# x's second chunk issued by ScalarE after its first chunk has landed, in a float32 adapter kernel with LayerNorm

## The reference

```python
h = einsum('bsh,bhk->bsk', x, W_down[r]) + b_down[r]     # 1024 -> 512
h = gelu(h, approximate=False)
u = einsum('bsk,bkh->bsh', h, W_up[r]) + b_up[r]         # 512 -> 1024
y = x + u
out = (y - mean(y)) * rsqrt(var(y) + 1e-5) * gamma[r] + beta[r]
```

## Time and profile before

| | |
|---|---|
| median of three runs | 362.9 us |
| the profiled execution's own time | 363.25 us |
| its span | 361.4 us |
| TensorE busy | 353.8 us (98%), 1547 matmuls |
| VectorE busy | 286.1 us (79%) |
| ScalarE busy | 183.5 us (51%) |
| chain that ended last | TensorE 98% |
| DMA moved | 96.59 MB, mean 267 GB/s |

### The profile page before, as it was taken

One profiled execution on the slowest core, in us unless ns is written; L12 is line 12 of the kernel. 1 busy time (PEld: TensorE's weight loads), 2 busy tenths in 40 slices (PEclk: granted clock), 3 DMA queues, 4 the chain that ended last, 5 costly groups with the idle time before them and its releaser, 6 DMA issues.

```text
span 361.4 us, 4953 instructions
## 1 busy us (share of the span) xinstructions
PE 353.8 (98%) x1547; PEld 290.1 (80%) x1547; DVE 286.1 (79%) x300; ACT 183.5 (51%) x299; POOL 59.0 (16%) x73
## 2 busy tenths in 40 slices
PE   9999999999999999999999999999999999999992
PEld 4888888888888888888888888888888888888881
DVE  3678989298993989849996699957989489893886
ACT  5675555761368414683256814476234862255131
POOL 0000232003220112202140022300232003320012
PEclk9999999999999999999999999999999999999998
DMA  6999999962999639994599926999198981645023
GB/s 206 392 409 408 409 347 364 358 248 79 323 331 365 237 125 363 321 355 171 171 358 344 340 122 234 350 346 356 49 301 335 380 319 51 239 147 203 1 116 116
DMA packets 27659, 96.59 MB, mean 267 GB/s; under 512 B 3202, under 2 KB 3714, under 8 KB 27650
## 3 DMA queue, kind: packets, MB, share of 16 engines
q1 hardware_dynamic: 23186, 81.27, 62.1%
q10 hardware_dynamic: 4464, 15.21, 10.8%
HBM read 79.70 MB, written 16.78 MB: 267 GB/s over the span
## 4 chain that ended last, share of the span: by engine, by line
PE 98%; DVE 1%; DVEq 0%; issue 0%
PE down_ps L296 48%; PE up_ps L303 48%; PE up_ps L410 1%; DVE h_full L670 0%; DVE rows L676 0%; DVE up_ps L653 0%; DVEq L43 0%; DVE last_mean L663 0%; DVE neg_shift L661 0%; DVEq L652 0%
## 5 line engine op out<-in xcount | busy, mean ns | idle before, releaser
L296 PE MATMUL down_ps<-x_hi,wd_hi 128*128 128x512 f32 x256 | 81.4, 391 | 0.0
L296 PE MATMUL down_ps<-x_lo,wd_hi 128*128 128x512 f32 x256 | 81.2, 390 | 0.0
L296 PE MATMUL down_ps<-x_hi,wd_lo 128*128 128x512 f32 x256 | 80.8, 389 | 0.0
L303 PE MATMUL up_ps<-wu_hi,h_hi 128*128 128x512 f32 x256 | 79.5, 389 | 0.0
L303 PE MATMUL up_ps<-wu_lo,h_hi 128*128 128x512 f32 x256 | 79.5, 389 | 0.0
L303 PE MATMUL up_ps<-wu_hi,h_lo 128*128 128x512 f32 x256 | 79.4, 389 | 0.0
L561 POOL TENSOR_TENSOR var_eps<-var,eps 128x1 f32<-128x1 f32 x31 | 22.8, 735 | 292.6 <-ACT squares L466 292.6
L463 ACT ACTIVATE neg_mean_scaled<-row_sum 128x1 f32<-128x1 f32 x31 | 6.3, 203 | 125.0 <-DVE rows L637 125.0
L625 DVE TENSOR_TENSOR h_lo<-h_full,h_hi 128x512 fp32r<-128x512 f32 x32 | 22.2, 692 | 47.7 <-ACT h_hi L458 47.7
L296 PEld LDWEIGHTS down_ps<-x_hi,wd_hi 128*128 128x128 f32 x256 | 48.3, 189 | 10.9 <-issue 0.8
L296 PEld LDWEIGHTS down_ps<-x_lo,wd_hi 128*128 128x128 f32 x256 | 48.3, 189 | 10.0
(11 more groups left out here) (45 smaller groups left out, 254.0 us busy)
## 6 DMA issues: line engine op xcount, KB each, us to landing
wu_stage<-W_up SPq DMA_DIRECT2D x32, 512.0 KB, 7.1
rows<-x SPq DMA_DIRECT2D x32, 512.0 KB, 7.3
x_stage<-xT SPq DMA_DIRECT2D x30, 512.0 KB, 6.7
wd_stage<-W_down SPq DMA_DIRECT2D x30, 512.0 KB, 8.1
out<-rows ACTq DMA_DIRECT2D x28, 512.0 KB, 4.0
b_up_row<-b_up SPq DMA_DIRECT2D x8, 512.0 KB, 4.5
gamma_row<-gamma SPq DMA_DIRECT2D x8, 512.0 KB, 9.4
beta_row<-beta SPq DMA_DIRECT2D x8, 512.0 KB, 10.2
```

The lines of the kernel that those rows point to most:

```text
L296: return pe.matmul(down_ps[:, kc, :], wd_part[:, n, c * K + kc * P:c * K + (kc + 1) * P], x_part[:, n, c * S:(c + 1) * S], start=start, st ...
L303: mm = pe.matmul(up_ps[:, t % 2, half], h_part[:, kc, t * P:(t + 1) * P], wu_part[:, kc, half], start=(kc == 0 and h_part is h_hi and wu_p ...
```

## The change

ScalarE no longer issues the load of x's second chunk right after that of the first. It issues it behind the unused Gelu, after a wait until x's first chunk has landed, and in front of the cast of the first chunk. Nothing else changes.

```diff
             act.dma_start(x_stage[:, 0, 0:S], x_src(0)[:, 0, 0:S]).then_inc(first_x_landed[0], 16)
-            act.dma_start(x_stage[:, 0, S:CPL * S], x_src(0)[:, 0, S:CPL * S]).then_inc(x_landed[0], 16)
             act.wait_ge(constants_ready, 2)
             act.activation(unused[:, :], eps[:, :], ACT.Gelu)
+
+            act.wait_ge(first_x_landed[0], 16)
+            act.dma_start(x_stage[:, 0, S:CPL * S], x_src(0)[:, 0, S:CPL * S]).then_inc(x_landed[0], 16)
             round_first(x_hi, x_stage, 0, slice(0, S), first_x_landed[0], first_x_hi)
```

## The result

The changed kernel takes 363.57 us (median of 22 runs, 363.08 to 364.73) against 362.83 us before (22 runs, 362.70 to 363.26): a ratio of 1.0022 with a 95% interval of 1.0016 to 1.0028. It is slower by 0.74 us, and its runs scatter three times as widely. The profiled execution of the changed kernel took 363.15 us, one of its faster ones, with a span of 361.3.

A forecast was written before the change was run, and what follows sets the result against it. TensorE, almost without a break, was taken as the bound. Terms of -0.05 (first matmul), 0, 0 and 0 to +0.1 (SyncE's parts) turned 362.9 us into 362.85, given as 362.9; range 362.5 to 363.6.

The forecast's parts named there:

- x's second chunk comes late: ScalarE's moved load: lands between about 6.4 and 6.95 us, both casts done by 8.3 at the latest; cost 0.
- 7.3 us point: Landing of x's second chunk from which it costs: two casts and handovers before the thirteenth matmul's weight load at 8.72.
- 5.1 us row: Profile row of x's fourth chunk on SyncE's queue, which took 5.1 us; used in rival 2.
- rival 2: x's second chunk lands too late, at 8.55; TensorE goes on at 9.94, 1.2 us late: 364.1 us; chance 0.1.
- SyncE's transfers beside and behind it: Transfers queued on SyncE delayed 0.7 us, bounds 0 and 1.12; cost 0, at the upper bound 0.1.
- The bounds 0.76 and 1.12 us: Delay of SyncE's queued transfers by x's 256 KB, at 343 GB/s and at the poorer 235 GB/s.
- my company row: Row of SyncE's x chunk issued at 4.05, which took 3.5 us; gives 6.95 for x's second chunk's landing.
- The issue in front of the first cast: DMA issue on ScalarE moves x_hi's first cast from 3.42 to about 3.9 us; cost 0.
- The cap on this gain: Warm-ups end at 5.40, so the first real matmul comes forward at most 0.15 us; gain taken as 0.05.
- Rival 3: TensorE's clock rises at another moment: 362.3 us if earlier, 363.5 if 1.3 us later; chance 0.06.

The follow-up runs named there:

- e7: The changed kernel with no edit, profiled a second time: 364.67 us.
- e8: The changed kernel with no edit, profiled a third time: 363.92 us.
- e1: The changed kernel with the issue of x's second chunk moved behind the cast of x's first chunk, without the wait: 363.60 us, ratio 1.0017.
- the second profile: The kernel before with no edit, profiled again: 362.77 us.
- e11: The kernel before with 8 instead of 11 warm-up matmuls: 364.50 us, ratio 1.0047.
- e2: The changed kernel without the wait; the issue of x's second chunk stays behind the unused Gelu: 362.82 us, ratio 1.0000.
- e13: The changed kernel with the wait on the unused Gelu's completion instead of the landing of x's first chunk: 363.12 us, ratio 1.0006.
- e14: The kernel of e13 with no further edit, profiled a second time: 363.01 us.
- e9: The changed kernel, with SyncE waiting for x's second chunk to land before it issues x's third chunk and all behind it: 363.69 us, ratio 1.0027.
- e12: The kernel of e9 with no further edit, profiled a second time: 365.22 us, span 361.9.

## Why the prediction was wrong

I gave 362.9, no difference to be told from the kernel before, with 0.88, and slower with 0.08. The difference is 0.74 us and is slower.

**The step that failed is the landing of the two chunks for the thirteenth matmul.** Two terms of the sum were put at nothing there. For "x's second chunk comes late" I let the landing lie between its own row (2.9 us) and one row in company (3.5 us), found both ahead of the 7.3 us point and set the term to 0. The 5.1 us row stood in the same group and went to rival 2 with a chance of 0.1, since that transfer had five others ahead of it. For "SyncE's transfers beside and behind it" I took +0.7 us with 1.12 as the bound, and a cost of 0, at most 0.1.

In four profiles with the issue at 3.4 us and SyncE's queue running (that of the result, e7, e8 and e1) x's chunk took 3.0, 5.5, 4.8 and 5.7 us, and W_down's second chunk, 3.2 and 2.8 us in the two profiles of before, took 4.3, 5.4, 4.8 and 5.6. In the first W_down's chunk alone makes the wait; in the other three both are late, and by the estimate above either alone would have cost. Which of them decides in the median run, no profile shows.

Rival 2 was right in direction and size: it has x's landing at 8.55, two casts and their handovers behind it, TensorE at 9.94 and 364.1 us. Measured are 8.94, 10.24 and 364.67 in one execution, 8.20, 9.51 and 363.92 in another. It left W_down's part out. The argument against it, that the chunk is alone on its own queue, is refuted by these two executions, in which it was alone there and took 5.5 and 4.8 us.

**The delays were read from mean rates.** The bounds 0.76 and 1.12 us came from the mean rate of a stretch, but a chunk counts as landed when its last packet is there. ScalarE's queue moved x's chunk in 144 packets. In the profile after, 142 were through by 6.0 us and 2 came from 6 to 7. In e7, 125 were through by 6.0; its queue from 6 to 7, then from 7 to 8:

```profile
q10 hardware_dynamic: 7, 0.01, 3.4%
...
q10 hardware_dynamic: 8, 0.01, 3.7%
```

The last 4 came after 8, and the chunk landed at 8.94. Most of the chunk was there by 6.0, and a few stragglers took nearly 3 us more. The mean rate doesn't show them.

**The slack was read from a slower execution than most, and the change itself shortens it.** The 0.35 us between the profiled execution (363.25) and the median of the runs stood in the prediction and wasn't used. It is TensorE's slow pace in the first 1.3 us of real work, absent in the second profile. Without it the thirteenth matmul is due at 8.47 instead of 8.94; with the first matmul at 5.37 instead of 5.67 it is due at 8.17. The prediction's 7.3 us point counted 1.39 us back from the weight load at 8.72, which runs ahead only where nothing waits; in e7 it starts at 10.21, right before the matmul. With the measured 1.3 us from landing to matmul, x's chunk costs from a landing at 7.64 on by the first profile, at 7.17 by the second, and at 6.87 in the changed kernel: even the 6.95 of my company row would have cost a little. For W_down's chunk the point is 8.17 - 0.79 = 7.38. In the profile after it landed at 7.97, 1.1 us later than in the first profile and so within my bound, and it cost 0.59 us all the same.

**With these the time adds up.** The time minus the start of the thirteenth matmul is 363.15 - 8.76 = 354.39, 363.92 - 9.51 = 354.41, 364.67 - 10.24 = 354.43 and, for e1, 364.83 - 10.41 = 354.42 with the late issue; for the kernel before it is 363.25 - 8.94 = 354.31 and 362.77 - 8.47 = 354.30. So in these executions one number decides. If it does in the median runs too, 363.57 stands for a start at 363.57 - 354.41 = 9.16, and 362.83 for 362.83 - 354.31 = 8.52: 0.64 us later, and 0.10 for taking up the work again, make the 0.74.

**What held.** The issue in front of the first cast costs nothing: it put the cast at 3.76 (3.9 predicted), and e1 without it is no faster. W_down's first columns gain about as estimated: they take 2.3 or 2.4 us in the eight profiles in which the whole of x's chunk goes out at 3.4 or after, and 2.5 to 2.7 in the five with it at 1.2; I had 0.1, bounds 0 to 0.3.

The cap on this gain was wrong. In all sixteen profiles the first real matmul starts 0.44 or 0.45 us behind the start of W_down's first cast, also in those whose warm-ups keep the slow pace to the end, and in e11, where they are long over: only one gate held it. So the first matmul comes forward from 5.56 and 5.67 to 5.37 to 5.43, worth 0.2 to 0.3 us by these starts and not 0.05. It is spent again at the thirteenth matmul. Rival 3's varying clock is real, but both kernels have it: it explains 0.5 us of scatter, and not the waits for a landing, at which the changed kernel loses its time.

The Trainium skill, page "DMA: Bandwidth & Descriptors", section "Rules for kernel authors", says to issue a DMA early and wait late. The four moments of issue bear it out here: 1.2 us 1.0000, 2.7 us 1.0006, 3.4 us 1.0022, 5.0 us 1.0157, the last with the clock's part in it.

## What to carry to other kernels

Read the landing of a moved transfer from all transfers of its size that are under way at the new time, and let the slowest of them set the bound at least; here the slowest neighbour's 5.1 us was itself exceeded, by 5.5 and 5.7. A wait ends with the last packet of the last operand. Look also at what the chain hides: here two operands of one matmul were late, and the chain names one. Before slack is taken from a profile, compare that execution with the median of the runs; where it is slower, its slack is too large. And count what the change itself takes from the slack: an earlier start makes every later operand due earlier. In this kernel the load was worth most at its old place, even though it landed 2 us before its use.

## What the runs showed that I had not expected

**Single packets can take three times as long.** SyncE's queue from 5.6 to 6.0 us (packets, MB, share of 16 engines), of the kernel before and then of the changed one:

```profile
q1 hardware_dynamic: 69, 0.13, 96.5%
...
q1 hardware_dynamic: 26, 0.05, 123.6%
```

Before, 69 packets took 96.5% of 16 x 0.4 us, 0.09 us each. In the changed kernel 26 packets took 123.6%, 0.30 us each (more than 100%, so a short stretch counts them only roughly). It isn't bound to the change or to this stretch: e7 has 0.14 us there, and the kernel before has 0.19 us from 7.2 to 7.6. What the runs show is when a whole 256 KB chunk of ScalarE's queue lands. Issued at 1.2 or 2.7 us it takes 2.9 to 3.5 us (before, e2, e13, e14); issued at 3.4 or 5.0 beside SyncE's queue, 3.0 to 6.5; at 3.4 with SyncE's further transfers held back, 3.1 and 3.2 (e9, e12). Which engine or memory makes single packets wait isn't shown by any run here; it stays open.

**The clock's rise moves between executions of one kernel** (compare with the second profile), and with three warm-ups fewer, and so a pause of 1.23 us before the first real matmul, it came only after 9 us, at a cost of 1.7 us. **A DMA issue overtakes the table load and the activation in front of it** on ScalarE: at 1.21 us in e2, with the table loading from 1.15 to 2.43 and the activation at 2.44. A wait on the activation's own semaphore holds it, to 2.68 in e13.
